# A four-layer transformer on one core: in the attention of layers 2 and 3, the transposed input of a batch is made at the head of the preceding batch's cycles instead of at the end of its first cycle

## The reference, cut to what matters

```
xn     = layernorm(x)                                   # rows of one batch: 112 x 256
q      = xn @ Wq.T + bq;   k, v = ctx @ Wk.T + bk, ctx @ Wv.T + bv
(layer 2: q, k = rope(q), rope(k))
probs  = softmax(q k^T / 4  (+ mask in layer 3))        # per head: 112 x 375
x      = x + tanh(g) * ((probs @ v) @ Wo.T + bo)
```

## Time and profile before

| | us |
|---|---|
| median of 3 timed runs (2767.16, 2767.51, 2771.26) | 2767.51 |
| the profiled execution, its own time | 2766.18 |
| its span, first to last instruction | 2764.4 |
| TensorE busy in the span | 2617.9 (95%) |
| VectorE, ScalarE, GpSimd busy | 1547.1 (56%), 1296.0 (47%), 642.0 (23%) |
| mean granted TensorE clock | 0.981 of full |

### The profile page before, as it was taken

The page is one execution under the profiler, slowest core; times in us unless marked ns, Lnnn a source line. Parts: engine busy times, 40 slices in busy tenths (PEclk is TensorE's granted clock), DMA queues, the critical chain, the costliest instruction groups (busy, mean ns, idle before and its releaser), DMA issues. The chain is left out here.

```text
span 2764.4 us, 56714 instructions
## 1 busy us (share of the span) xinstructions
PE 2617.9 (95%) x19818; PEld 1981.6 (72%) x19818; DVE 1547.1 (56%) x4177; ACT 1296.0 (47%) x3610; POOL 642.0 (23%) x626
## 2 busy tenths in 40 slices
PE   6999978999999999989899998999998999989998
PEld 4777756666666666656677766999995777768887
DVE  4777856555555555535787874333235887742222
ACT  4777743343434334331567663333335777732222
POOL 0666661000000000000444431222221111013232
PEclk9999989999999999999999999999999999999999
DMA  3000002000000000010000006999991000059897
GB/s 119 17 23 18 12 2 109 13 13 8 13 7 13 7 13 7 1 34 1 20 18 19 23 7 244 324 334 327 323 326 46 24 18 24 7 201 312 303 312 224
DMA packets 91811, 267.57 MB, mean 97 GB/s; under 512 B 25068, under 2 KB 50804, under 8 KB 77268
## 3 DMA queue, kind: packets, MB, share of 16 engines
q1 hardware_dynamic: 74356, 242.53, 25.4%
q0 software_dynamic: 13632, 18.62, 3.2%
q10 hardware_dynamic: 3616, 3.67, 0.4%
HBM read 248.13 MB, written 16.65 MB: 96 GB/s over the span
## 5 line engine op out<-in xcount | busy, mean ns | idle before, releaser
L825 PEld LDWEIGHTS a_full_ps<-ident,a_probs 112*125 112x125 f32 x2688 | 369.9, 190 | 122.6 <-issue 59.8
L1926 PEld LDWEIGHTS m_banks<-m_x_inT,m_w 128*128 128x128 f32 x3824 | 435.1, 192 | 15.2 <-issue 13.5
L1926 PE MATMUL m_banks<-m_x_inT,m_w 128*128 128x128 f32 x3824 | 442.2, 276 | 1.4 <-ACT m_x_inT L1997 0.9
L936 ACT ACTIVATE a_probs<-a_masked,a_negmax 112x375 f32<-112x375 f32 x512 | 305.4, 598 | 287.7 <-DVE a_negmax L1151 287.7
L825 PE MATMUL a_full_ps<-ident,a_probs 112*125 112x112 f32 x2688 | 417.5, 281 | 16.7 <-ACT a_pT L943 5.6
L1177 DVE COPY a_pT<-a_full_ps 125x448 f32<-125x448 f32 x448 | 277.4, 621 | 233.9 <-PE a_full_ps L825 231.9
L725 PE MATMUL a_full_ps<-attention_room 128*125 128x256 f32 (+1 forms) x960 | 330.0, 472 | 9.6 <-ACT a_qT L926 3.7
L717 PE MATMUL a_full_ps<-attention_room 128*128 128x375 f32 x896 | 325.0, 491 | 13.8 <-PEq L1769 8.6
L1151 DVE CUSTOM_DVE_ANT_0 a_masked<-a_sc_ps,a_mask_add 112x375 f32<-112x375 f32 x512 | 249.7, 544 | 33.2 <-PE a_sc_ps L812 32.0
L936 ACT ACTIVATE a_probs<-a_sc_ps,a_negmax 112x375 f32<-112x375 f32 x384 | 216.6, 575 | 89.4 <-DVE a_negmax L1157 89.3
L843 PEld LDWEIGHTS a_o_ps<-a_pT,a_v 125*32 125x32 f32 (+1 forms) x5376 | 165.2, 118 | 127.0 <-issue 98.7
(11 more groups left out here) (253 smaller groups left out, 3473.3 us busy)
## 6 DMA issues: line engine op xcount, KB each, us to landing
m_w<-in_L2f_w SPq DMA_DIRECT2D x105, 1024.0 KB, 6.4
m_w<-in_L3f_w SPq DMA_DIRECT2D x72, 768.0 KB, 5.9
attention_room<-in_ctxT SPq DMA_DIRECT2D x64, 375.0 KB, 3.1
m_w<-in_L3f_w SPq DMA_DIRECT2D x36, 640.0 KB
m_b<-in_L2f_b SPq DMA_DIRECT2D x35, 128.0 KB, 8.0
p_rows<-normed SPq DMA_DIRECT2D x16, 224.0 KB, 6.2
attention_room<-in_L0x_spline_wT SPq DMA_DIRECT2D x1, 2048.0 KB, 10.5
net_room<-in_L1f_w SPq DMA_DIRECT2D x2, 1024.0 KB
```

Of the source, the lines that this page charges most:

```text
L825: mm = pe.transpose(full_ps[0:KT, bank_of["turn", i, k], (j % 4) * S:(j % 4 + 1) * S], probs[:, i % 2, a, t * KT:(t + 1) * KT], ident[0:S, ...
L936: act.activation(probs[:, i % 2, a, 0:SK], src, ACT.Exp, bias=negmax[:, m:m + 1], scale=-1.0 if mask else 1.0, accum_out=rowsum[:, par, n: ...
L1926: mm = pe.matmul(ab_ps[:, (par * FC + f) % RING, i * SLOTS:(i + 1) * SLOTS], w[:, par, c, f * P:(f + 1) * P], x_inT[:, c, :], start=(c == ...
```

## The change

For layers 2 and 3 the table puts `xT` at the very head of a batch's cycles (ahead of the first turn of cycle 0). In layer 2 a `rest` moves, so that `k` 1 and what follows fall on other banks. In layer 3 `v` 0 goes from cycle 0 to cycle 2, and three `rest`s come in. So that the rows are there by then, the layernorm of batch t+2 is made in batch t: its statistics at the end of cycle 2 (layer 2) or cycle 0 (layer 3), and the rows at the end of cycle 3 or 1. Layer 1 keeps its table, but its `begin_norm` goes from ahead of the copies of cycle 2 to the end of that cycle. In layer 3 `divide_o` goes behind the copy of the second turn, in layers 2 and 3 the network's rows (L195) go from cycle 2 to cycle 3, on GpSimd `power` goes ahead of `spread`, and in layer 2 ScalarE's copy of `k` 1 in cycle 2 goes behind all four exponentials.

```diff
-    2: [[[], [("k", 0)], [], [("rest",), ("xT",)]],
+    2: [[[("xT",)], [("k", 0)], [], [("rest",)]],
         [[], [("q", 0)], [("out",), ("rest",)], []],
-        [[("rest",)], [("k", 1)], [("v", 0, 0)], []],
+        [[], [("k", 1)], [("v", 0, 0), ("rest",)], []],
         [[], [("v", 1, 0)], [("v", 2, 0)], [("rt",)]]],
-    3: [[[], [("k", 0)], [("v", 0, 0)], [("xT",)]],
-        [[], [("out",)], [("q", 0)], []],
-        [[], [("v", 1, 0)], [], []],
+    3: [[[("xT",)], [("k", 0)], [], [("rest",)]],
+        [[], [("out",)], [("q", 0)], [("rest",)]],
+        [[], [("v", 0, 0)], [("v", 1, 0)], [("rest",)]],
...
+    stats_at, rows_at = {1: (2, 0), 2: (2, 3), 3: (0, 1)}.get(layer, (None, None))
...
# ScalarE
                         groups = ahead(t, par, i)
+                        copies(t, par, i, 0)
                         for group in groups:
                             exps(*group, (0, 1))
                         if exists(t) and not copies_last:
                             copy_turn(t, i)
-                        if divided and (not copies_last or i >= 2):
+                        if divided and (not copies_last or i == NG - 1):
                             copies(t, par, i, 1)
...
# VectorE
-                        if layer == 2 and i == 0 and exists(t + 1):
-                            norm_apply(t + 1)
-                        if i == 0 and divided and not stats_last and exists(t - 1):
-                            divide_o(t - 1)
...
-                        if not stats_last and i == (0 if layer == 3 else 2) and exists(t + normed):
-                            begin_norm(t + normed)
...
-                        if i == 0 and stats_last and exists(t - 1):
+                        if i == 0 and divided and exists(t - 1):
                             divide_o(t - 1)
...
+                        if i == stats_at and exists(t + 2):
+                            begin_norm(t + 2)
+                        if i == rows_at and layer != 1 and exists(t + 2):
+                            norm_apply(t + 2)
-                        if i == 2 and early(t - 2) and not rows_by_gpsimd:
+                        if i == (NG - 1 if divided else 2) and early(t - 2) and not rows_by_gpsimd:
                             norm_net.apply(dve, t - 2, t - 2)
```

More of the change, by code:

```diff
@@ L300, in attention_stage @@
     copies_last = layer == 2
-    normed = 2 if layer != 3 else 1
-    stats_last = layer == 2
+    stats_at, rows_at = {1: (2, 0), 2: (2, 3), 3: (0, 1)}.get(layer, (None, None))
     by_scalar = 2 if copies_last else 0
@@ L662, in body @@
                 def body(t, par):
-                    if layer == 3 and exists(t + 1):
-                        power(t + 1)
                     if hd == 16 and isinstance(t, int) and t < 1:
@@ L672, in body @@
                         rope_q(t + 1)
+                    if layer == 3 and exists(t + 2):
+                        power(t + 2)
                     if early(t - 2):
                         net_rows(t - 2)
-                    if exists(t + 2) and layer != 3 and not stats_last:
+                    if layer != 3 and exists(t + 2):
                         power(t + 2)
@@ L683, in body @@
                         add_bias(0)
-                    if exists(t + 2) and stats_last:
-                        power(t + 2)
                     if isinstance(t, int) and t == 0:
                         core.clear_spent(pool)
-                if layer != 3:
-                    power(0)
+                power(0)
                 batches(pool, kan_body if kan else body, tail)
@@ L1029, in body @@
                         if copies_last:
-                            if i < 2:
+                            if i < NG - 1:
                                 copies(t, par, i, 1)
@@ L1337, in body @@
                         if i == 0 and exists(t + 1):
-                            if layer != 2:
+                            if layer == 1:
                                 norm_apply(t + 1)
@@ L1368, in body @@
                             row_stats(t - 1)
-                        if stats_last and i == NG - 1 and exists(t + 2):
-                            begin_norm(t + 2)
                 def kan_setup():
@@ L1385, in _ @@
                     norm_apply(0)
-                elif layer != 3:
+                else:
                     begin_norm(0)
+                    if layer != 1:
+                        norm_apply(0)
                 batches(dve, kan_body if kan else body, tail)
```

## The result

The changed kernel took 2786.16 us (median of four executions, 2785.12 to 2787.22), against 2767.57 for the kernel before, timed beside it. The ratio is 1.0063 with a 95% interval of 1.0048 to 1.0078: **slower by 0.63%**, which is 17 to 19 us. The forecast was 2786.0. A second set of five executions, taken later for the experiments, gave a ratio of 1.0065 (1.0052 to 1.0078).

A forecast was written before the change was run, and what follows sets the result against it. TensorE's own work was taken to set the pace. Layer 2 3.5, starts 2.3 and 0.8, and layer 3 12.6 sum to 19.2 on 2766.2: 2785.4, with 1.3 for the median about 2786; range 2766 to 2795.

The forecast's parts named there:

- Layer 2, cycle 0, +0.40: Layer 2, cycle 0: copying `xT` first and held VectorE rows delay exponentials, division and `pv` by 0.40 us a batch.
- Layer 2, cycle 2, -0.15: Layer 2, cycle 2: the scores' 0.24 wait goes, the third turn starts 0.09 later; gain 0.15 us a batch.
- Layer 3, +0.9 a batch: Layer 3, cycles 0 to 2: stalls of `pv`, `q` and `v` 1, less removed waits; +12.6 us over 14 batches.
- The lower bound: Layer 3 batches: if the stalls swallow each other, only that of `pv` counts, 0.4 - 0.33, about 0.
- The start of layer 3, +0.8: Start of layer 3: no products, `k` 0 now stands between `xT` and `q`; +0.8 us, between 0 and 3.
- The start of layer 2, +2.3: Start of layer 2: `xT` first makes `k` 0 3.6 us later, less GpSimd's idle 1.37; first scores 2.3 us later.
- Layer 1, at nothing: Layer 1: moving `begin_norm` (0.94 us) costs nothing, covered by long matmul work; without cover, up to 13 us.
- (a): Whole kernel: the waits go and nothing takes their place; 2758 us, chance 0.14.
- (b): Layers 2 and 3: gains and losses cancel; 2765 to 2772 us, chance 0.10.
- (c): Slower by half: `pv`'s stall hides part of `q`'s and layer 2 comes out even; 2776 us, chance 0.18.
- (d): Delays compound as each late copy makes the next exponentials late; up to 2800 us, chance 0.05.

The follow-up runs named there:

- VectorE's list and the memsets mended: Changed kernel with both divisions moved, layer 3's statistics and rows late, memsets behind the rows, both layer 2 rows early: 2759.35 us, 0.9977 against before.
- one of the mended kernels: Changed kernel with both divisions moved, layer 3's statistics and rows late, memsets behind the rows, without layer 2's early rows: 2762.57 us, 0.9985 against before.

## Why the prediction was right, and which terms were not

The total, its sign and its mechanisms were right; several terms were mis-sized, and their errors, +2.3, -3.6, and 1.5 that was not in it, cancelled. That the sum came within 0.2 us of the profile is luck; with the errors of one sign it would have been off by 7. (By the forecast's own sum, 2785.4 and 1.3 more, the last line should read 2786.7 and not 2786.)

- **Layer 2, cycle 0, +0.40 for the `xT` copy and the held rows.** The chain was right to its last link: undoing the link between shuffle and division removed the wait. Its size was 0.50. The copy's 0.34 measured 0.31 with the rows out of the way; what failed is "I take +0.40 for the two together". The maxima started at +1.49, not +1.35, because the row operation was held through two products of GpSimd (1.80 us), not to the end of the one that it met. With that cycle 0 to 1 gave +0.52 (4.91 and 5.63 us, 4.99 and 5.03 before).
- **Layer 2, cycle 2, -0.15.** 5.33 us after 5.48: as forecast. In sum +0.36 for a batch in the middle and +0.39 over the window of 14, 5.5 us where 3.5 stood.
- **Layer 3, +0.9 a batch.** Every stall that was named is there, each smaller: `pv` 0.17 for 0.39, `q` at +4.12 for +4.31, `v` 1 0.23 for 0.39. The step that was mis-sized is the first: the second turn was put at T - 0.96 and its copy at T - 0.34, and they were at T - 1.18 and T - 0.55. The copy follows its turn by 0.63, as assumed (0.62); it is the turn that stands earlier before the scores, in all batches alike, and everything behind it on VectorE moved up 0.2. Why the two turns and the way to the scores took 1.18 and not 0.96 is open. The distances from the maxima on, 1.79 and 0.57, held to the hundredth. 8.3 us where 12.6 stood. The lower bound, that the stalls swallow each other entirely, did not come.
- **The start of layer 3, +0.8, "there are no products".** There are no products, but two memsets and an addition, which hold VectorE's rows as well. The new rows of batch 1 stood right ahead of the scaled `q`, so the first scores came 3.1 late. By the first full batch it is 1.5, since the new order then runs 1.6 us quicker to that point. Moving the memsets gave back all of 3.1.
- **The start of layer 2, +2.3.** 2.6.
- **The drains.** The forecast had nothing there. Layer 2's end and the network behind it cost 3.0 (1.8 and 1.2), which is the clock. In layer 3 it went the other way: in the profile of before the clock was below full in the drain,

```profile
2410.00:2420.00 10.00, 8.14 (x89) 6.37 (x90) 6.43 (x21) 5.35 (x18) 0.94 (x2) 0.88 0.01 2
```

  and full there in after and with only layer 2 changed, whose layer 3 attention, in the old order, took 336.83 us, against 338.43 in before.
- **Layer 1, at nothing.** The moved statistics cost nothing: over 683 us from 20 us behind the stage's first matmul TensorE is busy 680.64 us before and 680.65 after. The end of that stage differs by 1.9 us between the two profiles of after (739.96 and 738.02 from its first matmul to the first of the network), again with the same instructions and another clock (0.50 and 0.67 from 1180 to 1190).
- **The rivals.** (a), faster, was to decide by maxima no later than 1.3 behind their scores in layer 3: they came at 1.76, and with the statistics and rows away that layer's batch was 20.21. But (a)'s 2758 was in reach of this order: with VectorE's list and the memsets mended it took 2759. (b), (c) and (d) fell by the time. Not settled by these runs is what the division ahead of the shuffle would do in the kernel before, which was not tried.

## What to carry to other kernels

Before an input is moved ahead, write down for each engine the list that it will stand in, and ask of every operation behind it who is waiting; here the change removed the waits that it was made for, and lost that gain and 17 to 19 us more, mostly on VectorE, where a division of 0.4 us stood behind the shuffle and 0.9 us of statistics stood ahead of the masked maxima. An operation that depends on nothing late (the division) is not to be left behind one that does (the shuffle). Where a difference is a few microseconds, divide it by stages first: 2 or 3 us here came from the clock in a drain, and looked like the effect of an edit that had moved nothing. And a profile is one execution: its mean granted clock is to be compared with those of the other executions of the same kernel.

## What the hardware showed that was not expected

- **A row operation of VectorE can be held through consecutive operations of GpSimd, not only the one that it meets.** 0.40 us alone; 0.78 beside one addition of 0.72; 1.45 beside a memset of 1.37; 1.80 beside two products (0.99, 0.85); 2.10 beside an addition and a memset (0.73, 1.38). The memset only writes, and holds as the others do. Statistics, 0.42, and the copies out of PSUM, 0.62, stayed as long as ever. The Trainium skill, page "SBUF — State Buffer", section "Who interferes with whom", says that the one that comes first has the shared ports for its whole instruction; the traces agree. At the two places of this change the waiting VectorE operation did not get in between two GpSimd operations that followed each other. That is not so everywhere: in layer 0 of before, the row operation of the earlier trace rows ended at 223.58, 0.14 behind the product that it met, although GpSimd's next operation had followed without a gap,

```profile
223.39 1.73 POOL L624 TENSOR_TENSOR a_sq<-a_near 128x896 f32<-128x896 f32 x1
```

  and so did the rows at the start of layer 2 of before (1.44 beside a memset of 1.38, with a product right behind it). In which case it gets in is open.
- **The same instructions met a different clock.** At the end of layer 2's attention the granted clock in one 10 us window was 0.50 (1.2 GHz) in after, in the kernel with layer 3's division first and in one of the mended kernels, 0.59 in the second profile of after, no lower than 0.83 in others, and 1.00 to the end in four. After, the kernel with layer 3's division first and the kernel with only layer 2 changed, which kept 1.00, have the same order of work in layer 2; so has the one with layer 3's statistics late, at 0.83. TensorE had been busy 8.10 of the 10 us of 1650 to 1660 in after, and 8.11 in the kernel with only layer 2 changed, whose clock did not fall. It cost up to 3.2 us. Executions of one and the same kernel differ too: in one set of before the time went from 2762.5 us at a mean of 0.983 to 2770.4 at 0.979, nearly 2 us for each thousandth. What decides it is open.
